# The second block of the experts' down weights as 48 rows: its own load, and a product over 48 partitions

## The reference, cut to what matters

```python
E, K, I = 16, 4, 176           # experts, experts per token, inner width; CAP = 128 tokens per expert
xg = xpad[buf]                                              # (16, 128, 256): tokens gathered per expert
gact = silu(einsum('ech,ehi->eci', xg, w_gate))             # inner width 176
mid = gact * einsum('ech,ehi->eci', xg, w_up)
eout = einsum('eci,eih->ech', mid, w_down) * wbuf[..., None]    # contraction over 176
y = zeros.at[buf].add(eout)                                 # back to the tokens, added
shared = silu(x @ sw_gate) * (x @ sw_up) @ sw_down          # inner width 352, every token
return y + shared
```

## Time and profile before

| | |
|---|---|
| median of three runs | 2037.52 us (2033.8 to 2038.13) |
| the profiled execution, its time | 2036.98 us |
| its span, first to last instruction | 2035.1 us |
| mean granted TensorE clock | 0.993 |
| instructions | 40453 |
| DMA: packets, MB | 58601, 73.46 |
| L740, the down products | 128 matmuls, mean 381 ns |
| loads of the down weights | 32 transfers, 256 KB each, median 5.0 us to landing |

### The profile page before, as it was taken

One profiled execution on the slowest core, in us unless ns is written; L12 is line 12 of the kernel. 1 busy time (PEld: TensorE's weight loads), 2 busy tenths in 40 slices (PEclk: granted clock), 3 DMA queues, 4 the chain that ended last, 5 costly groups with the idle time before them and its releaser, 6 DMA issues.

```text
span 2035.1 us, 40453 instructions
## 1 busy us (share of the span) xinstructions
PE 1954.4 (96%) x13825; PEld 1769.5 (87%) x13825; DVE 1423.7 (70%) x3588; ACT 1317.2 (65%) x3368; POOL 949.8 (47%) x974
## 2 busy tenths in 40 slices
PE   6988989898999999999999999999999999999999
PEld 4767867688899999999999999999999999998888
DVE  8348763554778777777877778687777868777753
ACT  4326623443778677776877777786777778676752
POOL 1642116534545536454553645455364545536242
PEclk9999989999999999999999999999999999999999
DMA  7752047700000000000000000000000000000000
GB/s 252 213 85 32 33 161 214 158 11 9 9 6 4 15 6 4 7 9 6 9 9 7 4 6 9 6 9 9 6 4 7 9 9 6 10 6 1 22 27 32
DMA packets 58601, 73.46 MB, mean 36 GB/s; under 512 B 9760, under 2 KB 45216, under 8 KB 58272
## 3 DMA queue, kind: packets, MB, share of 16 engines
q1 hardware_dynamic: 43808, 53.83, 8.1%
q0 software_dynamic: 14592, 17.04, 5.1%
HBM read 51.06 MB, written 19.80 MB: 35 GB/s over the span
## 4 chain that ended last, share of the span: by engine, by line
PE 62%; DVE 11%; ACT 9%; POOL 8%; issue 7%; DMA 2%; SPq 0%; ACTq 0%; POOLq 0%; DVEq 0%
PE phase_scores L1171 16%; PE phase_ring L1229 9%; PE phase_y L172 5%; PE phase_y L171 5%; PE phase_y L170 5%; PE phase_ring L170 4%; PE phase_ring L172 4%; PE phase_ring L171 4%; ACT phase_p L1203 3%; DVE phase_scores L1182 2%; POOL phase_rot L2387 2%; POOL phase_straight L2385 2%; PE phase_banks L170 1%; PE phase_banks L172 1%; PE phase_banks L171 1%
## 5 line engine op out<-in xcount | busy, mean ns | idle before, releaser
L1203 ACT ACTIVATE phase_p<-phase_scores,phase_bias 128x512 f32<-128x512 f32 (+3 forms) x680 | 417.5, 628 | 117.2 <-DVE phase_bias L1191 116.5
L1249 DVE TENSOR_TENSOR phase_pt_lo<-phase_ring,phase_pt_hi 128x512 fp32r<-128x512 f32 (+3 forms) x680 | 390.6, 603 | 89.7 <-ACT phase_pt_hi L1244 85.8
L1244 ACT ACTIVATE phase_pt_hi<-phase_ring 128x512 fp32r<-128x512 f32 (+3 forms) x680 | 343.0, 536 | 105.9 <-PE phase_ring L1229 102.7
L1229 PE MATMUL phase_ring<-sb_ident,phase_p 128*128 128x128 f32 x2312 | 341.0, 274 | 9.4 <-ACT phase_p L1203 4.5
L170 PE MATMUL phase_y<-phase_pt_hi,phase_v_hi 128*128 128x256 f32 (+1 forms) x1152 | 341.2, 296 | 6.7 <-DVE phase_y_lo L2361 6.7
L171 PE MATMUL phase_y<-phase_pt_lo,phase_v_hi 128*128 128x256 f32 (+1 forms) x1152 | 321.2, 279 | 0.0
L172 PE MATMUL phase_y<-phase_pt_hi,phase_v_lo 128*128 128x256 f32 (+1 forms) x1152 | 321.2, 279 | 0.0
L1229 PEld LDWEIGHTS phase_ring<-sb_ident,phase_p 128*128 128x128 f32 x2312 | 272.3, 141 | 50.2 <-ACT phase_p L1203 14.3
L1184 DVE TENSOR_REDUCE phase_peaks<-phase_scores 128x1 f32<-128x512 f32 (+1 forms) x408 | 265.8, 666 | 45.8 <-PE phase_scores L1171 43.5
L2385 POOL TENSOR_TENSOR phase_straight<-phase_rot,late_rope 64x512 f32<-64x512 f32 x128 | 163.9, 1281 | 275.1 <-ACT phase_rot L2254 275.0
L2402 POOL TENSOR_TENSOR sb_x<-sb_x,phase_part 128x512 f32<-128x512 f32 x128 | 165.0, 1289 | 252.7 <-ACT phase_part L2289 246.3
(11 more groups left out here) (272 smaller groups left out, 4870.7 us busy)
## 6 DMA issues: line engine op xcount, KB each, us to landing
phase_e_up<-expert_up SPq DMA_DIRECT2D x32, 352.0 KB, 4.8
phase_e_dn<-expert_down SPq DMA_DIRECT2D x32, 256.0 KB, 5.0
y_rows<-phase_zero SPq DMA_DIRECT2D x16, 512.0 KB, 7.9
sb_x<-y_rows POOLq DMA_DIRECT2D x16, 512.0 KB, 6.7
xn_rows<-phase_ln_xn SPq DMA_DIRECT2D x8, 512.0 KB, 3.0
late_raw_qk<-qk SPq DMA_DIRECT2D x16, 256.0 KB, 2.6
sb_x<-x SPq DMA_DIRECT2D x4, 512.0 KB, 5.8
phase_raw_up<-up SPq DMA_DIRECT2D x8, 256.0 KB, 3.6
```

The lines of the kernel that those rows point to most:

```text
L1203: act.activation(self.p[:, at:at + width], self.scores[:, at:at + width], ACT.Exp, bias=self.bias[:, t % 2:t % 2 + 1], accum_out=self.sums ...
L1229: done = pe.transpose(bank[:, j * P:(j + 1) * P], self.p[:, (4 * place + j) * P:(4 * place + j + 1) * P], self.core.ident[:])
L1244: act.activation(hi, value, ACT.Copy).then_inc(*self.t_hi.one)
L1249: dve.tensor_tensor(lo, value, as_f32(hi), ALU.subtract).then_inc(*self.t_lo.one)
```

## The change

The down weights of an expert are loaded by two transfers, one per block: 128 rows of 256 columns, and 48 rows of 256 columns. Both count on the same semaphore, and PE waits for the count of the second. The second block's product takes 48 partitions of both operands. Nothing writes or reads the other 80 rows of that block any longer. The padding on the host stays as it is.

```diff
         for n, key in enumerate(experts):
             self.up_in[n % self.SLOTS].plan([key])
-            self.down_in[n % self.SLOTS].plan([key])
+            self.down_in[n % self.SLOTS].plan([(*key, k) for k in range(IK)])
...
     def sp_expert(self, sp, n):
         s = n % self.SLOTS
         sp.dma_start(self.e_up[:, s], self.core.src["expert_up"][n]).then_inc(*self.up_in[s].one)
-        sp.dma_start(self.e_dn[:, s], self.core.src["expert_down"][n]).then_inc(*self.down_in[s].one)
+        for k in range(IK):
+            rows = self.e_rows(k)
+            sp.dma_start(self.e_dn[rows, s, k, :], self.core.src["expert_down"][n][rows, k, :]).then_inc(*self.down_in[s].one)
+
+    def e_rows(self, k):
+
+        return slice(0, min(P, I0 - k * P))
...
                 pe.wait_ge(*self.h_copied[tag, n])
-                pe.wait_ge(*self.down_in[n % self.SLOTS][tag, n])
+                pe.wait_ge(*self.down_in[n % self.SLOTS][tag, n, IK - 1])
...
                 for k in range(IK):
-                    done = pe.matmul(self.down_ps[n % 2], self.e_cols[:, n % 2, k * P:(k + 1) * P], self.e_dn[:, n % self.SLOTS, k, :],
+                    rows = self.e_rows(k)
+                    done = pe.matmul(self.down_ps[n % 2], self.e_cols[rows, n % 2, k * P:(k + 1) * P], self.e_dn[rows, n % self.SLOTS, k, :],
                                      start=k == 0, stop=k == IK - 1)
                 done.then_inc(*self.e_downed.one)
```

## The result

The changed kernel takes 2045.82 us (median of 6 runs, 2043.15 to 2047.61), the kernel before 2037.83 beside it (6 runs, 2033.8 to 2039.7). The ratio is 1.004, with a 95% interval of [1.003, 1.005]: slower by 8.0 us. The prediction said 2047.4 and +9.9.

A forecast was written before the change was run, and what follows sets the result against it. PE's own stream was taken to bound the experts' loops. Two changes of shape at 0.40 us per expert, 32 x 0.40 = 12.8, less 2.9 of gather waits, gave +9.9: 2047.4 us, range 2038 to 2052.5.

The forecast's parts named there:

- Bound: Experts' loops of both routed stages: the matmul engine's own stream sets the pace, 2.48 us per expert; additions lengthen the time.
- The marks: After the two stages: the first norm was to start 4.5 us later, SyncE's loads of 374.94 near 385.
- Going in, 0.20: Change from a 128-row to the 48-row product: a gap of 0.10 us plus 0.10 of weight load no longer hidden.
- Coming out, 0.19: Change from the 48-row product back to 128 rows: 0.13 us gap plus 0.06 of load shown before L729; 0.23 before a product.
- The pair, 0.40, and the period, 2.9: Both changes of shape cost 0.40 us per expert, 12.8 over 32; the loop's period goes from 2.48 to 2.9.
- The end of the range at 0.52: Upper bound per expert in us, if the array empties only after the modelled 0.38 instead of 0.22; gives 2052.2.
- Slack of 2.9 taken up: PE's waits for gathers of token rows, 1.9 us in the first stage and 1.0 in the second, absorb part of the cost.
- Loads: Down-weight transfers: four more issues per stage and the wait for both parts cost nothing; lighter traffic, worth 0 to 2.9 us, taken as 0.
- no gap: Rival: change of shape costs PE nothing, period stays 2.48, time 2037.5 us, or 2034.6 with every late gather in; chance 0.14.
- One side only: Rival: only one of the two changes of shape costs 0.20 us, +3.5 in all, time 2041.0 us; chance 0.10.
- The second part late: Rival: PE waits for the second down-weight transfer if landing exceeds 8.0 us; 2043.5 us at 9 us; chance 0.03.
- Clearly faster: Rival: the full 2.9 us of gather waits saved and 2.2 us of lower-clock stretches missed, time 2032.4 us; chance 0.05.

The follow-up runs named there:

- the pair with two visits: Against the changed kernel, down product in halves, entering and leaving the 48-row shape twice per expert: 2058.32 us; its control, all over 128 rows: 2035.06 us.

## Why the prediction was right

The direction, the mechanism and, nearly, the size hold, by its own steps. The forecast of +9.9 is 1.9 above the measured 8.0; 32 x 0.05 = 1.6 of that is the price of a pair of changes, taken at 0.40 where it is 0.35.

- *Bound.* PE's stream set the pace of the loop: what was added to it (0.35 per expert) came out at the end. The marks: the first norm came 3.6 later (4.5 said), and SyncE's loads at 383.33 (near 385 said).
- *Going in, 0.20.* Measured 0.19, as 0.09 of gap and 0.10 of load. The 16-row transposes priced it rightly, though they came from a 512-column product.
- *Coming out, 0.19.* This term was mis-sized: it measured 0.15. The gap is 0.09 and not 0.13. It came from the eight grouped transposes. Their last start was worked out rightly (29.37; the single record starts at 29.377). What was wrong is the 0.01 us taken for its 16 columns: the eight start 0.06 apart (0.45 for seven), so of the 0.136 from the last start to the load some 0.07 is a gap, and the estimate was about 0.06 too long. The load shown (0.055, said 0.06) was right. Where a product follows, 0.23 was said; with the blocks turned round that way out is 0.19 (0.09 of gap and 0.10 of load) and the pair 2.878 - 2.488 = 0.39.
- *The pair, 0.40, and the period, 2.9.* 0.35 and 2.83; 32 x 0.35 = 11.2 instead of 12.8. The end of the range at 0.52 (the array empty only after the modelled 0.38) was far off: a modelled end is no time at which the next thing could start.
- *Slack of 2.9 taken up.* L717's waits for gathers are gone. By stage, 16 x 0.35 = 5.6 less the measured 3.6 leaves 2.0 (1.9 said), and 5.6 less 8.4 - 3.7 = 4.7 leaves 0.9 (1.0 said); 3.7 is by how much the second stage began later. The sum would be 11.2 - 2.9 = 8.3, where 8.0 was measured. This term is the least certain one. The kernels with eight buffers say that the slack was not simply a gain to be had (1.1 us came in the first stage and none in the second, where other waits came), and in the pair with two visits nothing of it was seen.
- *Loads.* SyncE's four further issues and the wait for both parts cost nothing, as said. PE waits for no down weight. Product alone and both together differ by 2045.82 - 2044.21 = 1.6 us, the wrong way for a gain and inside the spread. Lighter traffic was taken at 0, with up to 2.9 the other way: no gain shows here, and near 2 where PE's stream isn't made longer.

Of the rivals, *no gap* fell by the loads with "issue" before them. *One side only* fell as well, for both sides have their 0.09. Its time of 2041.0 lies outside the 2043.15 to 2047.61 that was measured. *The second part late* fell with landings of at most 6.1 us. *Clearly faster* didn't come; its saving from lighter traffic shows only where the load is changed alone. The rule of the Trainium skill, page "TensorEngine Tiling (Array Packing)", section "Key Properties", that switching the mode requires a drain, agrees with the gaps in the traces for 32, 48 and 64 rows; for 96 rows the trace shows no gap. Whether it is this mode that changes with the number of rows, and what PE does in the 0.09 us, no trace here shows: shown is that the price comes with each change between a product over 128 rows and one over 64 or fewer. The other rule of the Trainium skill, page "TensorE: Matmul & The Clock Gate", section "Why this matters for your kernels", that a lone matmul with small K takes the same time as one with K=128, held for the matmul itself (376 ns with 48 rows, 379 with 128), and said nothing of its neighbours.

## What to carry to other kernels

Trimming the contraction of a product that stands alone between full ones buys nothing on PE: 256 columns streamed in 0.22 us over 48 rows as over 128. At 64, 48 and 32 rows it cost 0.35 us for the way in and out together. Pad such a block (96 rows were free here). Putting products of the same small shape next to each other should save changes too, since the two 48-row matmuls of an expert follow each other without a gap; no run tried it across experts. The load can still be trimmed by itself, if the padding is written once. When an edit looks free, look at what the next weight load was hidden under.

## What was not expected

- 96 rows cost nothing and 64 as much as 32 (records of 379, 428, 426 ns). The step lies between 64 and 96 rows, and the price below it hardly depends on the rows.
- Nearly half of the price is no gap at all (0.155 of 0.35): it is a weight load that lost its cover, 0.10 before a product and 0.055 before a turn.
- Doubling the number of products at half the width (128 columns) cost PE 2.51 instead of 2.48 us per expert, and nothing that shows in the kernel's time (2035.06): 128 columns in float32 still hide their loads.
- Two more gather buffers took away every wait for gathers and no time (2036.77 against 2037.32 us, a ratio of 1.0).
